# A two-layer transformer block on one core: score sums and exponential sums moved to TensorE, one PSUM bank for score and value sums, and the two streams of the second part without a gap

## The reference, cut to what matters

```python
x = L0_attn_x                                  # 8 sequences x 512 tokens x 128
# twice: layer 0, then layer 1, each with its own adaptive norm (sa, ca, ga, sb, cb, gb)
h = layernorm(x) * (1 + ca) + sa
x = x + ga * attention(h)
h = layernorm(x) * (1 + cb) + sb
x = x + gb * ffn(h)      # FP4 quantize/dequantize in blocks of 16, silu(gate) * up, down
```

```python
attn = einsum('bhtd,bhsd->bhts', q, k)                  # t and s run over 8
attn = (attn - max(attn)) * 32 + gate * position_bias   # q carries 1/32
probs = softmax(attn)
out = einsum('bhts,bhsd->bhtd', probs, v) @ Wo.T + bo
```

## Time and profile before

| | us |
|---|---|
| median of 3 runs | 1372.24 (1369.85 to 1372.98) |
| the profiled execution, its own time | 1373.02 |
| its span in the trace | 1371.2 |
| PE busy | 1128.8 (82%) |
| VectorE busy | 1057.5 (77%) |
| GpSimd busy | 930.0 (68%) |
| ScalarE busy | 625.6 (46%) |

### The profile page before, as it was taken

The page is one execution under the profiler, slowest core; times in us unless marked ns, Lnnn a source line. Parts: engine busy times, 40 slices in busy tenths (PEclk is TensorE's granted clock), DMA queues, the critical chain, the costliest instruction groups (busy, mean ns, idle before and its releaser), DMA issues. The chain is left out here.

```text
span 1371.2 us, 29825 instructions
## 1 busy us (share of the span) xinstructions
PE 1128.8 (82%) x10832; PEld 711.5 (52%) x10832; DVE 1057.5 (77%) x1468; ACT 625.6 (46%) x1217; POOL 930.0 (68%) x808
## 2 busy tenths in 40 slices
PE   5889999989999989999999996586657776856865
PEld 2245565645655645655655655354335554545654
DVE  4588968868878768779789776677797777789895
ACT  2245645536546446455456452345444343423332
POOL 3379878768788768798798773333578686684331
PEclk9699999999999989999999997688868886887988
DMA  5112112112111111121121120000000000000000
GB/s 151 35 36 59 37 32 60 41 27 56 41 44 41 37 40 47 36 54 43 28 56 43 31 57 21 8 1 1 0 0 0 1 1 1 0 8 9 9 16 23
DMA packets 48627, 42.17 MB, mean 31 GB/s; under 512 B 7869, under 2 KB 46808, under 8 KB 48472
## 3 DMA queue, kind: packets, MB, share of 16 engines
q1 hardware_dynamic: 48040, 39.36, 11.6%
q10 hardware_dynamic: 432, 0.79, 0.2%
HBM read 6.42 MB, written 2.10 MB: 6 GB/s over the span
## 5 line engine op out<-in xcount | busy, mean ns | idle before, releaser
L509 ACT ACTIVATE a_probs<-a_ps_s 128x512 f32<-128x512 f32 x512 | 303.8, 596 | 326.6 <-PE a_ps_s L417 322.4
L742 POOL TENSOR_TENSOR a_p_lo<-a_probs 128x512 f16<-128x512 f32 x384 | 419.0, 1113 | 34.2 <-ACT a_probs L509 31.8
L670 DVE TENSOR_REDUCE a_nmx<-a_ps_m 128x2 f32<-128x1024 f32 x256 | 311.4, 1217 | 34.6 <-PE a_ps_m L400 33.9
L433 PE MATMUL a_ps_o<-a_v_hi,a_probs 128*128 128x65 f16 x2048 | 244.1, 196 | 15.4 <-DVE a_p_lo L677 7.9
L434 PE MATMUL a_ps_o<-a_v_lo,a_probs 128*128 128x64 f16 x2048 | 241.4, 194 | 0.0
L435 PE MATMUL a_ps_o<-a_v_hi,a_p_lo 128*128 128x65 f16 x2048 | 241.1, 195 | 0.0
L433 PEld LDWEIGHTS a_ps_o<-a_v_hi,a_probs 128*128 128x128 bf16 x2048 | 189.9, 99 | 87.9 <-issue 58.9
L415 PE MATMUL a_ps_s<-a_qq,a_kk 128*128 128x512 f16 x512 | 198.0, 387 | 8.2 <-issue 5.3
L434 PEld LDWEIGHTS a_ps_o<-a_v_lo,a_probs 128*128 128x128 bf16 x2048 | 191.8, 99 | 25.1 <-issue 1.5
L417 PE MATMUL a_ps_s<-a_qq,a_k_l 65*128 65x512 f16 x512 | 198.3, 387 | 0.0
L435 PEld LDWEIGHTS a_ps_o<-a_v_hi,a_p_lo 128*128 128x128 f16 x2048 | 191.5, 98 | 0.0
(11 more groups left out here) (234 smaller groups left out, 2108.7 us busy)
## 6 DMA issues: line engine op xcount, KB each, us to landing
a_qq<-a_rhi SPq DMA_DIRECT2D x128, 128.0 KB, 2.4
a_qq<-a_rlo SPq DMA_DIRECT2D x128, 64.0 KB, 2.1
a_kk<-a_rhi SPq DMA_DIRECT2D x64, 64.0 KB, 2.0
a_k_l<-a_rlo SPq DMA_DIRECT2D x32, 64.0 KB, 2.1
out_x<-x_sb SPq DMA_DIRECT2D x8, 256.0 KB, 2.3
a_qq<-a_nmT SPq DMA_DIRECT2D x64, 2.0 KB
a_probs<-in_wq ACTq DMA_DIRECT2D x1, 512.0 KB, 5.1
a_wo<-in_wo SPq DMA_DIRECT2D x1, 512.0 KB, 12.3
```

The lines of the kernel that those rows point to most:

```text
L433: nc.tensor.matmul(out, hi, v_hi[:, b % 2, kt, g, 0:65], start=(kt == 0), stop=False)
L509: nc.scalar.activation(probs[:, p % 2, kt, h, :], ps_s[:, i % 2, :], ACT.Exp, scale=DH0 ** -0.5).then_inc(exp_done, 1)
L670: nc.vector.tensor_reduce(nmx[:, p % 2, i:2 * QT:QT], ps_m[:, n % 2, :, :], axis=X, op=ALU.max, negate=True).then_inc(free[n % 2], 1)
L742: nc.gpsimd.tensor_tensor(p_lo[:, p % 2, kt, h, :], pr, pr.bitcast(BF16)[:, 1:2 * L:2], ALU.subtract).then_inc(lo_pool, 1)
```

## The change

The sum of the score products moves from VectorE (SR) to PE (SS): the columns of the q and k weights and biases are stored with the 8 numbers of a head outermost, so that each of the 8 slices of 16 is summed by an accumulating matmul against the identity. Score sums and value sums share the bank `ps_o`, in the order in which they stand in the list, each half of four freed by `o_free`. VectorE adds the gate bias out of PSUM in two halves (SA). PE sums the exponentials (DS) into a bank of the ring, ScalarE copies them to `den`, and VectorE's DEN keeps only the reciprocal. `GAP` becomes 0, the round's items move in the ticks, and T1 moves ahead of the round's items and of C2 in its tick.

```diff
-STEP, GAP, NP = 7, 1, 3
+STEP, GAP, NP = 7, 0, 3
...
             elif kind == "SP":
                 for t in range(B):
-                    at(t0 + 9 + t, "SP", r, t)
-            elif kind == "SR":
+                    at(t0 + 9 + 3 * t // 4, "SP", r, t)
+            elif kind == "SS":
                 for t in range(B):
-                    at(t0 + 10 + t, "SR", r, t)
+                    at(t0 + 10 + 3 * t // 4, "SS", r, t)
+            elif kind == "SA":
+                for half in range(2):
+                    at(t0 + 13 + 3 * half, "SA", r, half)
             elif kind == "GATE":
-                at(t0 + 13, "GATE", r)
+                at(t0 + 12, "GATE", r)
             elif kind == "SM":
-                at(t0 + 18, "SM", r)
+                at(t0 + 16, "SM", r)
             elif kind == "PP":
                 for t in range(B):
-                    at(t0 + 19 + t, "PP", r, t)
+                    at(t0 + 17 + 3 * t // 4, "PP", r, t)
             elif kind == "PS":
                 for t in range(B):
-                    at(t0 + (20 if t < HB else 21) + t, "PS", r, t)
+                    at(t0 + 18 + 3 * t // 4, "PS", r, t)
+            elif kind == "DS":
+                at(t0 + 17, "DS", r)
             elif kind == "DEN":
-                at(t0 + 20, "DEN", r)
+                at(t0 + 18, "DEN", r)
             elif kind == "ON":
                 for half in range(2):
-                    at(t0 + 24 + 4 * half, "ON", r, half)
+                    at(t0 + 21 + 3 * half, "ON", r, half)
...
-                    at(t0 + 25 + 4 * half, "OT", r, half)
+                    at(t0 + 22 + 3 * half, "OT", r, half)
...
-                    at(t0 + 26 + 4 * half, "LY", r, half)
+                    at(t0 + 23 + 3 * half, "LY", r, half)
...
-                    at(t0 + 27 + 4 * half, "RES", r, half)
+                    at(t0 + 24 + 3 * half, "RES", r, half)
...
-    each(place_round, ("SM", "SR", "RES", "ON", "DEN"))
-    each(place_group, ("S2", "C2"))
-    each(place_round, ("LHT", "KVG", "OT", "LY", "PS", "LX"))
-    each(place_group, ("TD", "T1"))
+    each(place_round, ("SA", "SM", "RES", "ON", "DEN"))
+    each(place_group, ("S2", "T1", "C2"))
+    each(place_round, ("LHT", "KVG", "OT", "LY", "SS", "PS", "DS", "LX"))
+    each(place_group, ("TD",))
...
+                elif kind == "SS":
+                    r, t = it[1:]
+                    pe.wait_ge(s_mul, B * r + t + 1)
+                    wait_sums(t, it)
+                    for d in range(DH1):
+                        mm = nc.tensor.matmul(ps_o[:, t % HB, :], ident[:], s_prod[:, t % NP, :, d * H1:(d + 1) * H1],
+                                              start=(d == 0), stop=(d == DH1 - 1))
+                    mm.then_inc(s_sum, 1)
+                elif kind == "DS":
+                    r = it[1]
+                    pe.wait_ge(prob_ok, r + 1)
+                    for j in range(B):
+                        last = nc.tensor.matmul(bank[:, 0:B * H1], ident[:], prob[:, :, j, :],
+                                                start=(j == 0), stop=(j == B - 1))
...
+            def wait_sums(t, it):
+                if t % HB == 0 and (j := o_job[it[0], it[1], t // HB]) >= 1:
+                    pe.wait_ge(o_free, j)
...
                         act.wait_ge(p_mul, B * r)
+                        wait_full(act, ("DS", r - 1))
+                    nc.scalar.activation(prob[:], score[:], ACT.Exp).then_inc(prob_ok, 1)
+                elif kind == "DS":
+                    r = it[1]
+                    if r >= 1:
                         act.wait_ge(den_ok, r)
-                    nc.scalar.activation(prob[:], score[:], ACT.Exp).then_inc(prob_ok, 1)
+                    nc.scalar.activation(den[:].rearrange("p t h -> p (t h)"), bank[:, 0:B * H1],
+                                         ACT.Copy).then_inc(is_free(it), 1)
...
-                elif kind == "SR":
-                    r, t = it[1:]
-                    if t == 0 and r >= 1:
-                        dve.wait_ge(prob_ok, r)
-                    dve.wait_ge(s_mul, B * r + t + 1)
-                    nc.vector.tensor_reduce(score[:, t, :, :].rearrange("p s h -> p (s h)"),
-                                            s_prod[:, t % NP, :, :].rearrange("p s (h d) -> p (s h) d", d=DH1),
-                                            axis=X, op=ALU.add).then_inc(s_sum, 1)
+                elif kind == "SA":
+                    r, half = it[1:]
+                    part = slice(half * HB, (half + 1) * HB)
+                    if half == 0:
+                        dve.wait_ge(gbias_ok, r + 1)
+                        if r >= 1:
+                            dve.wait_ge(prob_ok, r)
+                    dve.wait_ge(s_sum, B * r + HB * (half + 1))
+                    nc.vector.tensor_tensor(score[:, part, :, :].rearrange("p t s h -> p t (s h)"), ps_o[:],
+                                            gbias[:, part, :, :].rearrange("p t s h -> p t (s h)"),
+                                            ALU.add).then_inc(o_free, 1)
...
-                    dve.wait_ge(prob_ok, r + 1)
-                    nc.vector.tensor_reduce(den[:], prob[:].rearrange("p t s h -> p t h s"), axis=X, op=ALU.add
-                                            ).then_inc(den_ok, 1)
-                    nc.vector.drain()
-                    nc.vector.reciprocal(rden[:], den[:])
+                    n = ring["DS", r]
+                    dve.wait_ge(free[n % 2], n // 2 + 1)
+                    nc.vector.reciprocal(rden[:], den[:]).then_inc(den_ok, 1)
```

More of the change, by code:

```diff
@@ L901, in second_part @@
     for it in order:
-        if it[0] in ("T1", "TD", "LHT", "KVG", "OT", "P"):
+        if it[0] in ("T1", "TD", "LHT", "KVG", "OT", "DS", "P"):
             ring[it] = len(ring)
@@ L905, in second_part @@
             y_job[(it[0],) + it[1:2] if it[0] == "TD" else it] = len(y_job)
-    prepared = [it for it in order if it[0] == "P"]
+    o_job = {}
+    for it in order:
+        if it[0] in ("SS", "PS") and it[2] % HB == 0:
+            o_job[it[0], it[1], it[2] // HB] = len(o_job)
     with ExitStack() as ex:
@@ L986, in second_part @@
         gb, gbs, pg_row = sb("gb", [1, 8]), sb("gbs", [1, 2]), sb("pg_row", [1, NG])
+        b_qk = sb("b_qk", [1, 2 * D])
         b_all, b_lo = sb("b_all", [1, NW]), sb("b_lo", [1, NW], FP16)
@@ L997, in second_part @@
             sem(n) for n in "guf sig gur r2 c2 n2 q2 h2T down xd".split())
-        y_full, y_free = sem("yf"), sem("yr")
+        y_full, y_free, o_free = sem("yf"), sem("yr"), sem("or")
         agg1, rstd1_ok, xhat1_ok, hT1_ok, kvg_ok, sig1_ok, gbias_ok = (
@@ L1045, in _ @@
                       (bo8[:], dram1["bo"].rearrange("(o n) -> o n", o=1).to_broadcast([B, D]))]
-            loads += [(b_all[:, k * D:(k + 1) * D], dram1[n].rearrange("(o n) -> o n", o=1))
-                      for k, n in enumerate(("bq", "bk", "bv"))]
+            loads += [(b_qk[:, k * D:(k + 1) * D], dram1[n].rearrange("(o n) -> o n", o=1))
+                      for k, n in enumerate(("bq", "bk"))]
+            loads += [(b_all[:, 2 * D:3 * D], dram1["bv"].rearrange("(o n) -> o n", o=1))]
             assert len(loads) == LOADS
@@ L1118, in item @@
                     pe.wait_ge(p_mul, B * r + t + 1)
-                    if t % HB == 0 and 2 * r + t // HB >= 1:
-                        pe.wait_ge(on_ok, 2 * r + t // HB)
+                    wait_sums(t, it)
                     for j in range(B):
@@ L1284, in item @@
                     elif it[1] == "qkv":
-                        nc.scalar.activation(w_all[:, 0:D], bank[:, 0:D], ACT.Copy, scale=q_scale)
-                        nc.scalar.activation(w_all[:, D:3 * D], bank[:, D:3 * D], ACT.Copy).then_inc(is_free(it), 1)
+                        for k in range(2):
+                            nc.scalar.activation(w_all[:, k * D:(k + 1) * D].rearrange("p (d h) -> p h d", h=H1),
+                                                 bank[:, k * D:(k + 1) * D].rearrange("p (h d) -> p h d", h=H1),
+                                                 ACT.Copy, scale=(q_scale, 1.0)[k])
+                        nc.scalar.activation(w_all[:, 2 * D:3 * D], bank[:, 2 * D:3 * D], ACT.Copy
+                                             ).then_inc(is_free(it), 1)
                         act.wait_ge(gws_ok, 1)
@@ L1294, in item @@
                         nc.scalar.activation(wo_t[:], bank[:, 2 * D:3 * D], ACT.Copy)
-                        nc.scalar.activation(b_all[:, 0:D], b_all[:, 0:D], ACT.Copy, scale=q_scale)
+                        for k in range(2):
+                            nc.scalar.activation(b_all[:, k * D:(k + 1) * D].rearrange("p (d h) -> p h d", h=H1),
+                                                 b_qk[:, k * D:(k + 1) * D].rearrange("p (h d) -> p h d", h=H1),
+                                                 ACT.Copy, scale=(q_scale, 1.0)[k])
                         nc.scalar.activation(pg_row[:], bank[0:1, 64:64 + NG], ACT.Copy).then_inc(is_free(it), 1)
```

(1 more changed line is left out.)

6 lines of the change are left out of this document (1 added, 5 removed).

## The result

The changed kernel takes 1392.05 us (median of four runs, 1389.85 to 1396.52); the kernel before, on the same chip, 1371.43 (four runs, 1369.85 to 1372.98). The ratio is 1.0155, with a 95% interval of 1.0136 to 1.0173: slower by 1.55%, where the forecast was slower by 0.4%. The direction is that of the forecast and the time lies in its range; the loss was put at under a third of what it is (5.8 of 20.6 us, each against the kernel before of its own set of runs). The profiled execution took 1389.85 us with a span of 1388.0.

The account below looks back on a forecast made before the run. VectorE and GpSimd, in order and waiting for each other, set the old round. First product at 1053.6, two rounds of 86, last stretch to 1308.9, tail 67.8: span 1376.7, forecast 1378 us against the median, range 1343 to 1404.

Parts of the forecast that it names:

- the prediction's clock zero: Start of the count for one round: the end of the first output projection (LY) of the round before.
- (1): TensorE at the round's start: last value sum, four turns with their down products, first score sum, 8.7 us.
- (2): GpSimd: three products, then the gate at 4.8 us, reaching 20.5; TensorE waits from 17 as one bank holds four sums.
- (3): VectorE from the first half addition through roundings and next group's scale to the maximum, 42.6; exponential out at 43.7.
- (4): ScalarE: exponential ahead of LX and the down step's copies; first copy out at 47.4, TensorE waits 13 us.
- (6): TensorE restarts at the lower clock after its wait: 2 us added, so a round takes 86 us.
- last stretch: From the last round's first product, 1225.6, to group 11's update, 1308.9: 83.3 us, where it was 112.5.
- tail: The stretch after group 11's update: 67.8 us as before, the same four groups of the same work.
- the restart: TensorE's slow start at 1.2 GHz after its wait for ScalarE's copy, priced at 2 us per round.
- Rival A: VectorE's relief wins: rounds keep 73 to 74 us, kernel 1344 us; chance 0.32.
- C: Rival: slower by clock and pieces, restart loses 5 us and sums on the path cost more; 1400 us, chance 0.15.
- (5): TensorE runs without a gap from the down step to the last projection: 32.7 us, reaching 80.1.

Follow-up runs that it names:

- e5: Changed kernel with its new ticks, but score products reduced on VectorE again and the gate added out of SBUF; 1393.73 us, ratio 1.0132.
- e1: Changed kernel with ScalarE's exponential one tick later, behind LX and the copies of the down step; 1373.64 us, ratio 1.0005.
- e4: Changed kernel with one matmul instead of eight for each score sum, so scores are wrong, all waits kept; 1386.87 us, ratio 1.0109.
- e2: Changed kernel with GpSimd's gate two ticks earlier, behind the third score product; 1384.37 us, ratio 1.0082.
- e6: Changed kernel with the denominators reduced on VectorE again, no sum of exponentials on TensorE; 1383.54 us, ratio 1.0062.
- e3: Changed kernel with T1, the turning of a group, back at the end of its tick behind the sums; 1388.85 us, ratio 1.0116.
- e8: Changed kernel with the first gate/up pair of groups 4 to 15 ahead of sums and projections in its tick; 1384.79 us, ratio 1.0086.
- c1: Changed kernel with the edits of e1, e2 and e3 together; 1370.49 us, ratio 0.9963 to the kernel before.
- c2: Changed kernel with the edits of e1, e2, e3 and e6 together; 1368.78 us, ratio 0.9952 to the kernel before.
- c3: c2 with gate and sigmoid one tick earlier, the pair of e8, and LX with its turning one tick later, behind the exponential; 1364.76 us, ratio 0.9943.
- c4: c3 with LX and its turns back where they were; 1367.64 us, ratio 0.9951 to the kernel before.
- e7: Changed kernel with the gap of seven ticks put back, groups 8 to 15 seven ticks later; 1401.93 us, ratio 1.0212.

## Why the prediction was right in direction and wrong in size

**Right, step by step.** The argument was that totals say faster and orders say slower, and that the orders decide. e5 (without the score sums on TensorE the whole loss is still there) and e1 (one tick takes 18 us back) bear this out, and e4 shows that the totals would have misled: TensorE's whole added load on the score sums is worth 5 us. The single terms, those marked z counted in the third round from the prediction's clock zero, here 1140.56:

| step | forecast | measured |
|---|---|---|
| (1) a score sum in pieces of 16 | 1.9 us | 1.95; two take 3.81 at 1147.91, two value sums 3.74 at 1196.44 |
| (2) gate | 4.8 | 4.7 (1157.68 to 1162.40) |
| (2), (3) TensorE waits for the addition | 4 | 5.7 |
| (3) VectorE's two roundings end (z) | 25.2 | 28.5 |
| (3) the scale of the next group | 6.8 | 3.6 |
| (3) the exponential is out (z) | 43.7 | 43.8 |
| (4) the first copy is out (z) | 47.4 | 47.3 |
| (4) TensorE has turned the hidden part (z) | 34 | 37.5 |
| (4) TensorE waits for the copy | 13 | 9.8 |
| (6) a round | 86 | 85.3, 85.4 |
| first round, up to the next first product | 82.3 | 83.1 |
| last stretch | 83.3 | 91.4 |
| tail | 67.8 | 73.8 |

That the exponential and the copy came out on time is luck in part. The gate came 1.4 us late, the second rounding took 3.77 us and not 1.61, and so VectorE had its products of gate and up 3.5 us late. The scale, which I had priced by its 6.8 us in the earlier trace rows, took 3.6 and gave 3.2 back. TensorE was 3.5 us later than forecast at its wait, among other things because the two sums behind its first wait took 5.87 us; I had counted a restart behind the second wait only. And in the first round's term the 2.0 us of the restart stand twice: the 82.8 for the next first product have them already. Counted once, the forecast for that round is 80.3, where 83.1 came, and the span 1374.7.

The gate took its short end: the like step took 0.45 us here and 1.84 in the earlier trace rows. In e2 VectorE was working during the gate, and the rows there separate the cases: 0.83 us beside the end of a VectorE instruction that multiplies two arrays, 0.45 beside the statistics. The Trainium skill, page SBUF — State Buffer, section Who interferes with whom, as weighed in the prediction, agrees with both rows.

Rival A, the relief of VectorE, falls: VectorE was relieved, and idle for 28 to 30 us of every round. C, which gave 1400, had its price wrong where the total came near (1392 is closer to it than to 1378): pieces cost nothing, and the mean clock of a round did not fall, it rose, from the 0.74 and 0.77 of the earlier trace rows to 0.88 to 0.90. After the wait of 9.8 us the down products start at half speed (1.65 us for six records, 0.83 or 0.91 usual), and the value sums from 1196.44 on are at full speed again. The Trainium skill, page TensorE: Matmul & The Clock Gate, section HAM oscillation, describes bursts behind waits that each start at the lower clock; the trace agrees for the start (1.65 us). That the whole run of (5) might stay there was my extension of it, and the trace does not bear it out.

**Wrong, by 11.3 us of span** (1376.7 against 1388.0). The start was 2.4 us early (969.0, not 971.35; 1.8 of it in the untouched first part), the first round 0.85 too long, two rounds together 1.3 too short. That is -2.8. The rest is two terms.

The last stretch, +8.1. The step that failed is "The last round lacks statistics, LX, two turns and projections (2.4 + 3.2 + 1.2 + 9.0 = 15.8)". The 15.8 were taken off the length of the round whole, as if the chain stayed on TensorE. VectorE and TensorE in the last round:

```profile
1277.74 0.95 DVE L1461 RECIPROCAL s_rden<-s_den 128x128 f32<-128x128 f32 x1 [8.55 <-ACT s_den L1290]
...
1288.22 3.39 DVE L1374 SCALAR_TENSOR_TENSOR s_r<-s_c,s_r 128x1408 f32<-128x1408 bf16 x1
...
1292.39 0.68 DVE L1469 TENSOR_TENSOR mod_bc<-s_ps_o,s_rden 128x512 f32<-128x512 f32 x1
```
```profile
1293.26 5.74 PE L1131 MATMUL s_ps_o<-s_p_prod,ident 128*128 128x128 f32 x32 [5.92 <-DVEq L1472]
```

Without the projections TensorE reaches the fifth value sum at 1287.3. The bank is freed only by VectorE's normalization (L1469), which stands 14.6 us behind the reciprocal, behind a scale, a rounding and an update of other groups. In the rounds before, the projections filled this time. The missed wait is 5.9 us, and the two sums behind it ran 2.0 us longer than the usual 3.74: 7.9 of the 8.1; smaller terms nearly cancel. This is read from the trace. No run takes this wait away alone; e6 bears on it: with the denominator on VectorE wait and sums are 2.2 us less and the stretch is 87.4, 4.0 less, but its full rounds are 1.9 to 3.1 shorter too.

The tail, +6.0. The step that failed is "67.8 us are left after it, the same four groups of the same work". The work is the same and its time is not. From one update of a group to the next the tail now takes 21.4, 17.8, 16.1 and 15.1 us, where it took 19.3, 17.5, 13.4 and 14.2. The third of these stretches, in the changed kernel and in e1, where it takes 13.4 as before:

```profile
1353.40:1369.50 16.10, 11.18 (x52) 7.88 (x52) 10.59 (x12) 6.23 (x11) 2.59 (x1) 0.89 0.06 18
```
```profile
1341.00:1354.40 13.40, 8.87 (x50) 6.42 (x49) 10.59 (x13) 5.00 (x10) 2.59 (x1) 1.00 0.07 21
```

VectorE and GpSimd do the same 10.59 and 2.59 us; TensorE is busy 2.3 us longer at a clock of 0.89 instead of 1.00. The same pair of gate/up products, in the changed kernel and in e1, and VectorE ahead of it in the changed kernel:

```profile
1359.21 4.07 PE L1097 MATMUL s_ps_gu<-w_gu,s_hqT 128*128 128x352 f32 x8 [2.62 <-DVE s_h L1409]
```
```profile
1345.53 2.63 PE L1099 MATMUL s_ps_gu<-w_gu,s_hqT 128*128 128x352 f32 x8 [2.77 <-DVE s_h L1411]
```
```profile
1355.40 1.63 DVE L1372 SCALAR_TENSOR_TENSOR s_r<-s_c,s_r 128x1408 f32<-128x1408 bf16 x1 [1.33 <-ACT s_c L1242]
```

Waits of like length precede both, so what granted one the full clock and not the other is not settled by these rows. The slower pair makes 1.4 of the 2.7 us. The other 1.3 are VectorE's wait for ScalarE's rounding, which e1 does not have: ScalarE's copy and rounding came late behind down products that ran slower as well (the last twelve records 2.47 us, 1.71 in e1). So the clock accounts for the 2.7 us, but not by the mean of the stretch: in e3, e8 and c1 to c4 this stretch has 0.88 and takes 14.2 to 14.7 us (14.7 in e8, which leaves T1 in its new place). In the fourth stretch, 0.9 us longer, six records of the down products take 1.49 us where they took 0.99, behind the same wait of 8.32 us. The score sums are not the cause: e5, which has none on TensorE, has the same four stretches to a tenth (21.5, 17.7, 16.1, 15.1).

For the 2.1 of the first stretch, the round's last residual now comes at 1316.7, after group 11's update and 1.9 us waited, where it came 7 us before it. With the gap back (e7) this stretch takes 18.9 us and the tail 68.4, so the longer first stretch goes with the missing gap; how much of it is that residual stays open.

Two of the signs that I named were wrong as well. VectorE "under 45 us per round" is 55.5: I had taken 19 to 20 us, waits among them, off the busy time of 63.9, of which only 9.7 are reductions and 1.9 the denominator, and two additions of 0.7 came for one of 1.2. And the clock was to be at 7 to 8 tenths and was 0.88 to 0.90. Of the signs named for being wrong, two came: the stretch after group 11 took 73.8 us and not 68, and the first product stood at 969.0 and not 971. The missing gap, "worth no fixed time", is worth 8 to 10 us in the whole (e7); it was in the sum, but inside the 29 us of the last stretch, of which 21 came.

**What stays open.** Why the gains of the single moves do not add is shown for one pair only (the denominator and the exponential, c2). What bounds a round of c3 at 78.6 us I can't name; its waits are short and many. Score sums in a bank of their own, which would remove the first wait without moving the gate, weren't tried.

## What to carry to other kernels

When engines work in order through one list that is written by hand, look at what stands behind a moved item on every engine, not only on the one that does its main work: here one exponential, a tick too early on ScalarE, cost 18 of 20 us (14.6 of them in the rounds and the last stretch, 4.5 in the tail, which holds no exponential). Compare stretches before spans: the untouched first part alone ends up to 6 us apart from trace to trace. Relieving the busiest engine gains nothing where waits set the pace, and added work is nearly free where it fills a wait. When a stage with less work is forecast, don't subtract the missing work from the old chain; follow the chain of each engine again, because the next one takes over.

## What the runs showed of the hardware

- The same work of four engines in one stretch of the tail took 13.4 us at a granted clock of 1.00 and 16.1 us at 0.89, but 14.2 to 14.7 us at 0.88 in six other kernels: the mean clock of a stretch did not give its length.
- The same code of the first part ended between 849.0 and 855.3 us in fourteen traces of one execution each.
- Taking matmuls away lowered the clock of what stayed: the mean of the third round fell from 0.90 to 0.82 in e4, and a gate/up pair took 4.69 us instead of 2.53.
- An accumulating sum whose moving operand is eight pieces of 16 numbers takes the 1.95 us of one with 128 in a row.
- A table load of 1.28 us on ScalarE cost nothing where ScalarE waited before its exponential, and stood on the path in e1, where copies ran up to it.
